# Layernorm scalars and V evictions on ScalarE instead of VectorE, and a second PSUM bank for the Q projection

## Chip, cores and metric

One Trainium2 chip, all 8 cores. The metric is the device time in microseconds of the slowest core, for one launch.

## What is computed

One layer on x of 4 x 4096 x 1024: a layernorm without weights, causal attention with 16 heads of 64, and a gated feed-forward network of hidden size 3072 on the same normalised input, whose output gates the attention's.

```python
def _layernorm(x, axis=-1, eps=1e-5):
    m = jnp.mean(x, axis=axis, keepdims=True)
    v = jnp.var(x, axis=axis, keepdims=True)
    return (x - m) / jnp.sqrt(v + eps)

q = split_heads(x @ Wq) + pos[None, None]
k = split_heads(x @ Wk) + pos[None, None]
v = split_heads(x @ Wv)
scores = jnp.einsum('bhqd,bhkd->bhqk', q, k) * DIM_K ** (-0.5)   # causal mask, softmax
out = jnp.einsum('bhqk,bhkd->bhqd', attn, v)                     # then @ Wo

h = jax.nn.silu(x @ wg.T) * (x @ wu.T)                           # then @ wd.T

xn = _layernorm(x, axis=-1)
s = attention(xn)
g = _silu(ffn(xn))
x = x + s * g
```

## The kernel before

Two cores share one batch element. Each computes 2048 of its 4096 query rows (four blocks of 512, `QBS`, interleaved so that the causal work is alike) and all of its keys and values. Activations are bf16 with the contracted dimension on the partitions; sums are fp32 in PSUM.

The program is a list of instructions for each engine, in an order written out by hand: `P.op(engine, ...)` appends to one engine's list, `waits` names the semaphore counts that it waits for, and each engine runs its list strictly in that order. "T" is TensorE, "V" VectorE, "S" ScalarE, "G" GpSimd's DMA queue, "SY" SyncE's. So an instruction that waits holds up all that stands behind it on its engine. `P.flush` ends a stage.

Stages, in order:
- b0: `ln_phase` normalises the core's 16 own tiles of 128 rows into `xn_own`.
- f1: gate and up projection, with the weights transposed on TensorE. f2: down projection; the gate silu(ffn) goes to HBM by way of `xstA` (`g_spill`).
- b34: `ln_phase` again, for the 32 key/value tiles into `xn_kv`. After each tile a callback, `b34_cb`, appends up to three units of other work from a sorted queue: for each of the 8 head pairs (two heads of 64 are one 128-column pair) four Q units and a last row of squares, and for head pair 0 eight K units, eight norm units, 32 V units and one `u_bound`.
- b5: attention for head pairs 0 to 7. In each pair, block j of four runs over 8, 16, 24 or 32 key chunks of 128 (`EXT`). A chunk c is two score matmuls (`emit_sc`, L916, into bank pair `SC2[c % 2]`), one exp of 128x1024 on ScalarE (L930), on the last four chunks of a block two mask multiplications on VectorE (L944), and, two chunks later, two value matmuls (`emit_av`, L963). After every odd chunk, and after the last `emit_av` of a block, one unit of the next pair's `kv_units` is popped from `fillers`; what is left of them is drained at the end of the pair.
- b6: output projection, gating and residual.

A layernorm tile (`ln_phase`): VectorE sums x (L304) while ScalarE squares it (L307) into a PSUM buffer of 128x1024 that all tiles share (in b34 it is `AV2`); VectorE sums the squares (L310); four VectorE instructions on 128x1 columns of `sLN` give mean, squared mean, mean square and variance (L313 to L322); ScalarE does ln and exp(-0.5 ln) (L325, L328); VectorE makes -mean*rstd (L331) and scales the tile (L335); TensorE transposes it in eight matmuls (L350); ScalarE copies them out in two (L357).

A Q unit (`q_qs`) is eight matmuls of 128x512 into the one bank `Qps[0]` (L609) and an addition of the position table on VectorE (L616); the next unit's first matmul waits for that addition. Each later unit then does `q_sq` for the unit before: squares on VectorE (L627), a matmul with a column of ones (L632), a maximum on VectorE (L641).

A V unit (`emit_vc`) is eight matmuls of 128x128 (L791) into bank c % 2 of `KV2` and a copy of 128x128 to `Vaug` on VectorE (L798). `u_bound` is four VectorE instructions on 1x4 (L811 to L821), four small matmuls (L827) and four additions to the exp's bias table `sBM` (L836), for which the first exp of the next pair waits.

At a block's end ScalarE takes ln and exp(-1) of each head's row of sums (L988, L995), TensorE spreads them (L1002), VectorE copies them (L1011) and multiplies (L1019).

Of the kernel before, what the change touches and what calls it, by code (L numbers as in the profile page):

```python
# [172 lines left out]
def build_program(cfg):  # L173
# [40 lines left out]
    with ExitStack() as top:  # L214
# [55 lines left out]
        def ln_phase(xt_src, ntile, xn_dst, dsem, gates, tag, pool_ext=None,  # L270
                     xnt_ext=None, xnt_gate=None,
                     tp_gate=None, sq_gate=None, interleave_cb=None,
                     tps_ext=None, sqb_ext=None):
            with ExitStack() as ph:
                pe = ph.enter_context
                if pool_ext is not None:
                    xst, xnt = pool_ext
                else:
                    xst = [pe(nc.sbuf_tensor(f"xst{tag}{i}", [128, E], F32))
                           for i in range(2)]  # L280
                    xnt = xnt_ext if xnt_ext is not None else [
                        pe(nc.sbuf_tensor(f"xnt{tag}{i}", [128, E], BF16))
                        for i in range(2)]
                Tps = tps_ext if tps_ext is not None else [
                    pe(nc.psum_tensor(f"Tps{tag}{i}", [128, GT * 128], F32))
                    for i in range(2)]
                sqb = sqb_ext if sqb_ext is not None else pe(
                    nc.psum_tensor(f"sqb{tag}", [128, E], F32))
                xst_free = [None, None]
                sq_free = sq_gate  # L290
                xnt_free = [xnt_gate, xnt_gate]
                tp_free = [tp_gate, tp_gate]
                chain = [None, None]
                last_ev = None
                tile_toks = []
                tctr = 0
                for n in range(ntile):
                    par = n % 2
                    w = [xst_free[par]] + (gates if n < 2 else [])
                    tdma = P.op("SY", ld(xst[par][:], xt_src[n]),  # L300
                                waits=w, inc=dsem[par], amt=16)
                    L = sLN[par]
                    t1 = P.op("V", lambda v, L=L, b=xst[par][:]:
                              v.reduce_sum(L[:, 0:1], b, axis=AX.X),  # L304
                              waits=[tdma, chain[par]], inc="sV")
                    t2 = P.op("S", lambda s, a=sqb[:], b=xst[par][:]:
                              s.activation(a, b, AF.Square),  # L307
                              waits=[tdma, sq_free], inc="sS")
                    t3 = P.op("V", lambda v, L=L, a=sqb[:]:
                              v.reduce_sum(L[:, 1:2], a, axis=AX.X),  # L310
                              waits=[t2], inc="sV")
                    sq_free = t3
                    t4 = P.op("V", lambda v, L=L: v.tensor_scalar(  # L313
                        L[:, 2:3], L[:, 0:1], 1.0 / E, None, ALU.mult),
                        waits=[t1], inc="sV")
                    t5 = P.op("V", lambda v, L=L: v.tensor_tensor(
                        L[:, 3:4], L[:, 2:3], L[:, 2:3], ALU.mult),
                        waits=[t4], inc="sV")
                    t6 = P.op("V", lambda v, L=L: v.tensor_scalar(
                        L[:, 4:5], L[:, 1:2], 1.0 / E, None, ALU.mult),  # L320
                        waits=[t3], inc="sV")
                    t7 = P.op("V", lambda v, L=L: v.tensor_tensor(  # L322
                        L[:, 5:6], L[:, 4:5], L[:, 3:4], ALU.subtract),
                        waits=[t5, t6], inc="sV")
                    t8 = P.op("S", lambda s, L=L: s.activation(  # L325
                        L[:, 6:7], L[:, 5:6], AF.Ln, bias=sCV[:, 0:1]),
                        waits=[t7, tok_consts], inc="sS")
                    t9 = P.op("S", lambda s, L=L: s.activation(  # L328
                        L[:, 7:8], L[:, 6:7], AF.Exp, scale=-0.5),
                        waits=[t8], inc="sS")  # L330
                    t10 = P.op("V", lambda v, L=L: v.tensor_scalar(  # L331
                        L[:, 3:4], L[:, 2:3], L[:, 7:8], -1.0, ALU.mult, ALU.mult),
                        waits=[t9], inc="sV")
                    t11 = P.op("V", lambda v, L=L, a=xnt[par][:], b=xst[par][:]:
                               v.tensor_scalar(a, b, L[:, 7:8], L[:, 3:4],  # L335
                                               ALU.mult, ALU.add),
                               waits=[t10, xnt_free[par]], inc="sV")
# [27 lines left out]

        with ExitStack() as phb0:
# [178 lines left out]
            with ExitStack() as phc:  # L545
# [27 lines left out]
                KV2 = pc(nc.psum_tensor("KV2", [128, max(2 * KVPD, E)], F32))  # L573
                AVps = [AV2[0:65, 0:QBS], AV2[0:65, AVPD:AVPD + QBS]]
                KVp = [KV2[:, 0:KW], KV2[:, KVPD:KVPD + KW]]
                Qps = [SC2[0][:, 0:QW]]
                SQp1 = SC2[0][0:1, 512:512 + QW]
                wq_free = [None, None]
                qps_free = [None]
# [16 lines left out]
                def q_qs(p, qs):  # L596
                    par = p % 2
                    qd = qst[par]
                    last = None
                    for ec in range(EC):  # L600
                        w = [qd["tw"], tok_xnown, qps_free[0]]
                        if p == 0 and qs == 0 and ec == 0:
                            w += [tok_f2S, tok_f1V]
                        last = P.op(
                            "T", lambda t, o=Qps[0][:],
                            l=Wsl[par][:, ec, :],
                            r=xn_own[:, ec, qs * QW:(qs + 1) * QW],
                            st=(ec == 0), sp=(ec == EC - 1):
# [2 lines left out]
                    wq_free[par] = last  # L611
                    tev = P.op("V", lambda v,
                               o=Q_all[:, p, qs * QW:(qs + 1) * QW],
                               a=Qps[0][:],
                               b=sPQ[:, qs * QW:(qs + 1) * QW]:
                               v.tensor_tensor(o, a, b, ALU.add),  # L616
                               waits=[last, tpq], inc="sV")
                    qps_free[0] = tev
                    qd[("tev", qs)] = tev

                def q_sq(p, qs):
# [58 lines left out]
                def kv_units(p, ks, vs, xw):  # L680
# [96 lines left out]
                    def emit_vc(c):  # L777
# [4 lines left out]
                        for ec in range(EC):  # L782
                            w = [kv["twv"], xt, st["kvb"][bi]]
                            if ec == 0:
# [6 lines left out]
                                t.matmul(o, l, r, start=st_, stop=sp),  # L791
                                waits=w,
                                inc="sT" if ec == EC - 1 else None)
                        tev = P.op("V", lambda v,
                                   o=Vaug[par][:, c, :, 0:64],
                                   i_=bank[:, 0:128].rearrange(
                                       "p (two sv) -> p two sv", two=2):
                                   v.tensor_copy(o, i_),  # L798
                                   waits=[last, st["vread"][par]],
                                   inc="sV")  # L800
                        st["kvb"][bi] = tev
                        if c == KVC - 1:
                            st["sl_free"][vs] = last
# [53 lines left out]
                def b34_cb(n, toks):  # L857
                    holder["toks"] = toks
                    c = 0
                    while (qpos[0] < len(b34q) and b34q[qpos[0]][0] <= n  # L860
# [8 lines left out]
                    xnt_ext=[Kp[1][:, i * E:(i + 1) * E]  # L869
                             for i in range(2)],  # L870
                    xnt_gate=tok_f2T,
                    tp_gate=tok_f2S, sq_gate=tok_f1V,
                    tps_ext=[SC2[1][:, 0:GT * 128],
                             SC2[1][:, GT * 128:2 * GT * 128]],
                    sqb_ext=AV2[:, 0:E],
                    interleave_cb=b34_cb)
                while qpos[0] < len(b34q):
                    b34q[qpos[0]][1]()
# [271 lines left out]
```

How the kernel before makes its waits and increments, by code:

```python
            def body(eng):  # L152
                hw = self.hw[qn]
                for fn, waits, inc, amt in ops:
                    for (sn, val) in waits:
                        if val > hw.get(sn, 0):
                            eng.wait_ge(self.sems[sn][0], val)
                            hw[sn] = val
                    ins = fn(eng)
                    if inc is not None:
                        ins.then_inc(self.sems[inc][0], amt)
```

## Time and profile before

| | us |
|---|---|
| median of 2 runs | 2556.6 (2509.32 and 2603.88) |
| the profiled execution | 2511.39 |
| its span, slowest core (core 2) | 2509.8 |
| the other cores' spans | 2493.0 to 2507.1 |

Of the span TensorE matmuls are busy 70%, ScalarE 38%, VectorE 33%. These are means over six stages with different limits, so each stage is to be read by itself. All times of rows below are microseconds from the start of the span, on core 2. The two runs lie 95 us apart; all of what follows is read in, and compared with, the profiled execution, which is like the faster one.

### The profile page before, as it was taken

How to read it: one execution, taken by the hardware profiler on the slowest of the kernel's cores; microseconds unless marked ns; L12 is line 12 of the kernel's file. 1: busy time of each engine (PE TensorE's matmuls, PEld its weight loads, DVE VectorE, ACT ScalarE, POOL GpSimd, SP SyncE). 2: the span in 40 equal slices, each digit the busy share in tenths (PEclk: the TensorE clock that was granted, in tenths of full speed). 3: DMA queues.
4: the chain of work that ended last, by engine and by line, in shares of the span. 5: the costliest groups of instructions: out<-in, count | busy, mean ns of one | idle time of the engine just before them, and what ended most of it. 6: DMA issues, size and time to landing. Idle time of an engine off the chain costs nothing. (4 is left out here: it accounts for less than half of the span.)

```text
span 2509.8 us, 25986 instructions; the slowest of 8 cores (2493.0 to 2509.8 us)
## 1 busy us (share of the span) xinstructions
PE 1748.9 (70%) x8990; PEld 729.5 (29%) x9088; DVE 825.9 (33%) x1746; ACT 958.8 (38%) x1125; POOL 87.4 (3%) x135
## 2 busy tenths in 40 slices
PE   1178888989983444443688777877877787776752
PEld 0134444444431221222223232332323233221211
DVE  4533333330003444444333324233332423321133
ACT  3311111111001111112475665857566584767500
POOL 0011101000000000000000000000000000000000
PEclk9999999999996666665888888988888898888986
DMA  2153433320115121111200000000000000020155
GB/s 77 59 63 39 50 38 47 42 26 34 51 51 88 38 51 42 34 42 42 30 1 5 5 5 4 1 9 1 5 5 5 0 1 1 1 34 1 51 178 173
DMA packets 75135, 89.85 MB, mean 36 GB/s; under 512 B 52994, under 2 KB 53122, under 8 KB 74882
## 3 DMA queue, kind: packets, MB, share of 16 engines
q0 software_dynamic: 62768, 45.62, 11.7%
q1 hardware_dynamic: 12242, 42.57, 5.3%
q8 instruction: 77, 1.26, 0.2%
q14 instruction: 48, 0.39, 0.1%
HBM read 100.24 MB, written 16.78 MB: 47 GB/s over the span
## 5 line engine op out<-in xcount | busy, mean ns | idle before, releaser
L930 ACT ACTIVATE BIG<-SC,sBM 128x1024 bf16<-128x1024 f32 x640 | 683.9, 1111 | 322.5 <-PE SC L916 247.2
L963 PE MATMUL AV<-BIG 128*65 128x512 bf16 x1280 | 421.0, 412 | 87.5 <-DVE BIG L944 36.9
L916 PE MATMUL SC<-BIG 64*128 64x512 bf16 x1280 | 261.8, 414 | 1.3 <-PEq L164 1.3
L488 ACT ACTIVATE sSG<-Gps 128x512 bf16<-128x512 f32 x96 | 57.3, 597 | 378.7 <-PE Gps L474 378.7
L791 PE MATMUL KV<-BIG 128*128 128x128 bf16 x2048 | 182.3, 245 | 25.3 <-DVE BIG L1011 19.9
L474 PE MATMUL Gps<-RA,wgT 128*128 128x512 bf16 x752 | 194.6, 403 | 1.3 <-issue 0.4
L798 DVE CAST BIG<-KV 128x128 bf16<-128x128 f32 x256 | 75.1, 293 | 346.5 <-PE KV L791 343.4
L484 PE MATMUL Ups<-RA,wuT 128*128 128x512 bf16 x744 | 180.4, 381 | 1.3
L963 PEld LDWEIGHTS AV<-BIG 128*65 128x65 bf16 x1280 | 103.2, 115 | 238.9 <-issue 228.9
L350 PE MATMUL SC<-sID,BIG 128*128 128x128 bf16 x256 | 32.4, 306 | 197.4 <-DVE BIG L335 191.5
L528 PE MATMUL Dps<-BIG 128*128 128x512 bf16 x752 | 165.1, 379 | 2.4 <-PEq L164 1.5
L791 PEld LDWEIGHTS KV<-BIG 128*128 128x128 bf16 x2048 | 143.2, 111 | 80.4 <-issue 77.3
L493 DVE TENSOR_TENSOR BIG<-sSG,Ups 128x512 bf16<-128x512 bf16 x96 | 66.0, 688 | 282.2 <-PE Ups L484 278.6
L944 DVE TENSOR_TENSOR BIG<-BIG,sTRI 128x512 bf16<-128x512 bf16 x256 | 97.5, 422 | 177.8 <-ACT BIG L930 177.8
L714 PE MATMUL KV<-BIG 128*128 128x512 bf16 x484 | 142.5, 443 | 19.5 <-DVE BIG L1011 7.8
L916 PEld LDWEIGHTS SC<-BIG 64*128 64x128 bf16 x1280 | 59.6, 94 | 269.4 <-issue 269.3
L325 ACT ACTIVATE sLN<-sLN,sCV 128x1 f32<-128x1 f32 x48 | 14.1, 294 | 313.8 <-DVE sLN L322 313.8
L474 PEld LDWEIGHTS Gps<-RA,wgT 128*128 128x128 bf16 x768 | 77.7, 103 | 94.0 <-issue 15.8
L1092 PE MATMUL OPs<-BIG,RA 128*128 128x512 bf16 x250 | 71.1, 448 | 47.6 <-DVE ot L1109 42.8
L484 PEld LDWEIGHTS Ups<-RA,wuT 128*128 128x128 bf16 x768 | 76.2, 99 | 94.3 <-issue 6.6
L609 PE MATMUL SC<-RA,BIG 128*128 128x512 bf16 x248 | 91.7, 534 | 14.7 <-DMA BIG<-Wq 8.3
L528 PEld LDWEIGHTS Dps<-BIG 128*128 128x128 bf16 x768 | 75.1, 98 | 92.4 <-issue 2.0
(79 smaller groups left out, 1258.5 us busy)
## 6 DMA issues: line engine op xcount, KB each, us to landing
xstA<-x_q SPq DMA_DIRECT2D x32, 512.0 KB, 4.4
xstb<-x_kv SPq DMA_DIRECT2D x32, 512.0 KB, 3.9
g_spill<-xstA POOLq DMA_DIRECT2D x16, 512.0 KB, 2.9
gt<-g_spill POOLq DMA_DIRECT2D x16, 512.0 KB, 5.9
out<-ot SPq DMA_DIRECT2D x16, 512.0 KB, 3.0
wgc<-wg POOLq DMA_DIRECT2D x24, 256.0 KB, 4.0
wuc<-wu POOLq DMA_DIRECT2D x24, 256.0 KB, 5.4
wdc<-wd POOLq DMA_DIRECT2D x24, 256.0 KB, 5.5
```

Of the source, the lines that this page charges most:

```text
L474: t.matmul(o, l, r, start=st, stop=sp),
L484: t.matmul(o, l, r, start=st, stop=sp),
L528: t.matmul(o, l, r, start=st, stop=sp),
L609: t.matmul(o, l, r, start=st, stop=sp),
L714: t.matmul(o, l, r, start=st_, stop=sp),
L791: t.matmul(o, l, r, start=st_, stop=sp),
L798: v.tensor_copy(o, i_),
L916: t.matmul(SC2[bi][:, h * QBS:(h + 1) * QBS], Kp[par][h * 64:(h + 1) * 64, c * 128:(c + 1) * 128], Q_all[h * 64:(h + 1) * 64, p, j * QBS:( ...
L930: s.activation(expb[bi], SC2[bi][:, 0:2 * QBS], AF.Exp, scale=cfg.SM, bias=sBM[par][:, col:col + 1]),
L944: v.tensor_tensor(expb[bi][:, h * QBS:(h + 1) * QBS], expb[bi][:, h * QBS:(h + 1) * QBS], sTRI[:, r * QBS:(r + 1) * QBS], ALU.mult),
L963: t.matmul(AVps[h][:], Vaug[par][:, c, h, :], expb[bi][:, h * QBS:(h + 1) * QBS], start=st_, stop=sp),
L1092: t.matmul(OPs[op][:, ew * EW:(ew + 1) * EW], AO[:, rc, q2 * 128:(q2 + 1) * 128], Wo_sb[:, rc, ew * EW:(ew + 1) * EW], start=st_, stop=sp),
```

## The change

Three edits.

1. In `ln_phase` the five VectorE instructions on 128x1 become ScalarE activations: mean, squared mean, 1e-5 minus the squared mean, mean square, then ln with that difference as its bias, exp, minus the mean, and its product with rstd: six new ScalarE instructions for five VectorE ones. The buffer of squares becomes two, and in b34 they are the SBUF tiles `xstA` (free once the last `g_spill` is stored) and no longer `AV2`.
2. `Qps` has two banks in turn, the second in `AV2`.
3. The copy of a V unit (L798) is a ScalarE copy.

```diff
-                sqb = sqb_ext if sqb_ext is not None else pe(
-                    nc.psum_tensor(f"sqb{tag}", [128, E], F32))
+                sq = sq_ext if sq_ext is not None else [
+                    pe(nc.psum_tensor(f"sqb{tag}{i}", [128, E], F32))
+                    for i in range(2)]
...
-                              waits=[tdma, sq_free], inc="sS")
+                              waits=[tdma, sq_free[par]], inc="sS")
...
-                    t4 = P.op("V", lambda v, L=L: v.tensor_scalar(
-                        L[:, 2:3], L[:, 0:1], 1.0 / E, None, ALU.mult),
-                        waits=[t1], inc="sV")
-                    t5 = P.op("V", lambda v, L=L: v.tensor_tensor(
-                        L[:, 3:4], L[:, 2:3], L[:, 2:3], ALU.mult),
-                        waits=[t4], inc="sV")
-                    t6 = P.op("V", lambda v, L=L: v.tensor_scalar(
-                        L[:, 4:5], L[:, 1:2], 1.0 / E, None, ALU.mult),
-                        waits=[t3], inc="sV")
-                    t7 = P.op("V", lambda v, L=L: v.tensor_tensor(
-                        L[:, 5:6], L[:, 4:5], L[:, 3:4], ALU.subtract),
-                        waits=[t5, t6], inc="sV")
+                    t4 = P.op("S", lambda s, L=L: s.activation(
+                        L[:, 2:3], L[:, 0:1], AF.Copy, scale=1.0 / E),
+                        waits=[t1], inc="sS")
+                    t5 = P.op("S", lambda s, L=L: s.activation(
+                        L[:, 3:4], L[:, 2:3], AF.Square),
+                        waits=[t4], inc="sS")
+                    t5b = P.op("S", lambda s, L=L: s.activation(
+                        L[:, 5:6], L[:, 3:4], AF.Copy, scale=-1.0, bias=1e-5),
+                        waits=[t5], inc="sS")
+                    t6 = P.op("S", lambda s, L=L: s.activation(
+                        L[:, 4:5], L[:, 1:2], AF.Copy, scale=1.0 / E),
+                        waits=[t3], inc="sS")
                     t8 = P.op("S", lambda s, L=L: s.activation(
-                        L[:, 6:7], L[:, 5:6], AF.Ln, bias=sCV[:, 0:1]),
-                        waits=[t7, tok_consts], inc="sS")
+                        L[:, 6:7], L[:, 4:5], AF.Ln, bias=L[:, 5:6]),
+                        waits=[t5b, t6], inc="sS")
...
-                    t10 = P.op("V", lambda v, L=L: v.tensor_scalar(
-                        L[:, 3:4], L[:, 2:3], L[:, 7:8], -1.0, ALU.mult, ALU.mult),
-                        waits=[t9], inc="sV")
+                    ta = P.op("S", lambda s, L=L: s.activation(
+                        L[:, 3:4], L[:, 2:3], AF.Copy, scale=-1.0),
+                        waits=[t9], inc="sS")
+                    tb = P.op("S", lambda s, L=L: s.activation(
+                        L[:, 5:6], L[:, 3:4], AF.Copy, scale=L[:, 7:8]),
+                        waits=[ta], inc="sS")
...
-                Qps = [SC2[0][:, 0:QW]]
+                Qps = [SC2[0][:, 0:QW], AV2[:, 0:QW]]
...
-                        w = [qd["tw"], tok_xnown, qps_free[0]]
+                        w = [qd["tw"], tok_xnown, qps_free[qp]]
...
-                        tev = P.op("V", lambda v,
+                        tev = P.op("S", lambda s_,
                                    o=Vaug[par][:, c, :, 0:64],
                                    i_=bank[:, 0:128].rearrange(
                                        "p (two sv) -> p two sv", two=2):
-                                   v.tensor_copy(o, i_),
+                                   s_.copy(o, i_),
                                    waits=[last, st["vread"][par]],
-                                   inc="sV")
+                                   inc="sS")
...
-                    tp_gate=tok_f2S, sq_gate=tok_f1V,
+                    tp_gate=tok_f2S, sq_gate=gdone,
...
-                    sqb_ext=AV2[:, 0:E],
+                    sq_ext=[xstA[0], xstA[1]],
```

## Rows read from the trace of the kernel before

**Rows 1.** Windows, by stage: window, length, busy us (instructions) per engine, TensorE clock, DMA.
```profile
10.10:134.00 123.90, 16.75 (x134) 12.99 (x135) 61.26 (x128) 41.38 (x81) 4.06 (x6) 1.00 0.26 69
...
751.50:1200.70 449.20, 186.53 (x862) 89.49 (x879) 199.71 (x426) 81.47 (x161) 9.83 (x12) 0.63 0.20 47
1200.70:2363.40 1162.70, 914.77 (x4928) 335.13 (x4948) 363.49 (x888) 759.62 (x769) 13.12 (x15) 0.86 0.05 6
```
**Rows 2.** Groups by line: count, busy us, mean ns of one, idle before.
```profile
L930 ACT ACTIVATE BIG<-SC,sBM 128x1024 bf16<-128x1024 f32 x640 | 683.9, 1111 | 322.5 <-PE SC L916 247.2
L798 DVE CAST BIG<-KV 128x128 bf16<-128x128 f32 x256 | 75.1, 293 | 346.5 <-PE KV L791 343.4
L609 PE MATMUL SC<-RA,BIG 128*128 128x512 bf16 x248 | 91.7, 534 | 14.7 <-DMA BIG<-Wq 8.3
L357 ACT CAST BIG<-SC 128x512 bf16<-128x512 f32 x64 | 34.4, 589 | 69.5 <-PE SC L350 69.5
```
**Rows 3.** Timeline of one layernorm tile in b0: start, length, engine, line.
```profile
47.39 1.23 DVE L310 TENSOR_REDUCE sLN<-sqba 128x1 f32<-128x1024 f32 x1 [1.91 <-ACT sqba L307]
...
49.37 0.29 ACT L325 ACTIVATE sLN<-sLN,sCV 128x1 f32<-128x1 f32 x1 [2.08 <-DVE sLN L322]
49.75 0.20 ACT L328 ACTIVATE sLN<-sLN 128x1 f32<-128x1 f32 x1
...
50.45 0.81 DVE L335 TENSOR_SCALAR BIG<-xstA,sLN 128x1024 bf16<-128x1024 f32 x1 [0.18 <-DVE sLN L331]
```
**Rows 4.** Waits in b34 and in b5: engine, line, releaser, us in total, times, longest.
```profile
PE SC L609 <- DVE BIG L616: 5.2, 5, 1.4
...
ACT BIG L930 <- DVE sBM L836: 73.0, 7, 10.7
```
**Rows 5.** Timeline of b34: second of two adjoining Q units.
```profile
939.35 1.89 PE L609 MATMUL SC<-RA,BIG 128*128 128x512 bf16 x8 [0.95 <-DVE BIG L616]
```
**Rows 6.** Timeline of b34: a V unit ahead of a row of squares.
```profile
803.97 1.06 PE L791 MATMUL KV<-BIG 128*128 128x128 bf16 x8
...
805.13 0.29 DVE L798 CAST BIG<-KV 128x128 bf16<-128x128 f32 x1 [2.23 <-PE KV L791]
...
805.90 0.58 PE L632 MATMUL SC<-BIG,sONE 128*1 128x512 bf16 x1 [0.88 <-DVE BIG L627]
```
**Rows 7.** Timeline of b34's end: the last V unit and u_bound.
```profile
1199.11 0.24 PE L827 MATMUL KV<-sBSB,sOR 1*128 1x1 bf16 x4 [1.46 <-DVE sBSB L821]
```
**Rows 8.** Timeline of attention, two chunks with a V unit (head pair 0).
```profile
1318.04 2.12 ACT L930 ACTIVATE BIG<-SC,sBM 128x1024 bf16<-128x1024 f32 x2 [0.16 <-PE SC L916]
...
1318.87 0.62 PE L791 MATMUL KV<-BIG 128*128 128x128 bf16 x8
...
1320.35 2.12 ACT L930 ACTIVATE BIG<-SC,sBM 128x1024 bf16<-128x1024 f32 x2 [0.19 <-PE SC L916]
```
**Rows 9.** Timeline of attention, the same two chunks without one (head pair 7).
```profile
2263.31 2.12 ACT L930 ACTIVATE BIG<-SC,sBM 128x1024 bf16<-128x1024 f32 x2 [0.16 <-PE SC L916]
...
2265.59 2.12 ACT L930 ACTIVATE BIG<-SC,sBM 128x1024 bf16<-128x1024 f32 x2 [0.16 <-PE SC L916]
```
**Rows 10.** Timeline of a block's end with a V unit.
```profile
1295.19 0.61 PE L791 MATMUL KV<-BIG 128*128 128x128 bf16 x8
1295.45 0.59 ACT L988 ACTIVATE sRCF<-AV 1x512 f32<-1x512 f32 x1 [1.70 <-PE AV L963]
```
**Rows 11.** Timeline of a head pair's end.
```profile
1346.10 1.40 DVE L1019 TENSOR_TENSOR RA<-AV,BIG 64x512 bf16<-64x512 f32 x2
...
1346.14 4.99 PE L791 MATMUL KV<-BIG 128*128 128x128 bf16 x48 [1.72 <-DVE BIG L1011]
...
1351.56 0.22 DVE L811 TENSOR_SCALAR sMK<-sMQ,sMK 1x4 f32<-1x4 f32 x1
...
1352.92 0.23 PE L827 MATMUL KV<-sBSB,sOR 1*128 1x1 bf16 x4 [1.79 <-DVE sBSB L821]
...
1354.05 2.12 ACT L930 ACTIVATE BIG<-SC,sBM 128x1024 bf16<-128x1024 f32 x2 [10.48 <-DVE sBM L836]
```

More of the change, by code:

```diff
@@ L272, in ln_phase @@
                      tp_gate=None, sq_gate=None, interleave_cb=None,
-                     tps_ext=None, sqb_ext=None):
+                     tps_ext=None, sq_ext=None):
             with ExitStack() as ph:
@@ L286, in ln_phase @@
                     for i in range(2)]
-                sqb = sqb_ext if sqb_ext is not None else pe(
-                    nc.psum_tensor(f"sqb{tag}", [128, E], F32))
+                sq = sq_ext if sq_ext is not None else [
+                    pe(nc.psum_tensor(f"sqb{tag}{i}", [128, E], F32))
+                    for i in range(2)]
                 xst_free = [None, None]
-                sq_free = sq_gate
+                sq_free = list(sq_gate) if sq_gate else [None, None]
                 xnt_free = [xnt_gate, xnt_gate]
@@ L305, in ln_phase @@
                               waits=[tdma, chain[par]], inc="sV")
-                    t2 = P.op("S", lambda s, a=sqb[:], b=xst[par][:]:
+                    t2 = P.op("S", lambda s, a=sq[par][:], b=xst[par][:]:
                               s.activation(a, b, AF.Square),
-                              waits=[tdma, sq_free], inc="sS")
-                    t3 = P.op("V", lambda v, L=L, a=sqb[:]:
+                              waits=[tdma, sq_free[par]], inc="sS")
+                    t3 = P.op("V", lambda v, L=L, a=sq[par][:]:
@@ L310, in ln_phase @@
                               v.reduce_sum(L[:, 1:2], a, axis=AX.X),
                               waits=[t2], inc="sV")
-                    sq_free = t3
-                    t4 = P.op("V", lambda v, L=L: v.tensor_scalar(
-                        L[:, 2:3], L[:, 0:1], 1.0 / E, None, ALU.mult),
-                        waits=[t1], inc="sV")
-                    t5 = P.op("V", lambda v, L=L: v.tensor_tensor(
-                        L[:, 3:4], L[:, 2:3], L[:, 2:3], ALU.mult),
-                        waits=[t4], inc="sV")
@@ L319, in ln_phase @@
-                    t6 = P.op("V", lambda v, L=L: v.tensor_scalar(
-                        L[:, 4:5], L[:, 1:2], 1.0 / E, None, ALU.mult),
-                        waits=[t3], inc="sV")
-                    t7 = P.op("V", lambda v, L=L: v.tensor_tensor(
-                        L[:, 5:6], L[:, 4:5], L[:, 3:4], ALU.subtract),
-                        waits=[t5, t6], inc="sV")
+                    sq_free[par] = t3
+                    t4 = P.op("S", lambda s, L=L: s.activation(
+                        L[:, 2:3], L[:, 0:1], AF.Copy, scale=1.0 / E),
+                        waits=[t1], inc="sS")
@@ L330, in ln_phase @@
                         waits=[t8], inc="sS")
-                    t10 = P.op("V", lambda v, L=L: v.tensor_scalar(
-                        L[:, 3:4], L[:, 2:3], L[:, 7:8], -1.0, ALU.mult, ALU.mult),
-                        waits=[t9], inc="sV")
+                    ta = P.op("S", lambda s, L=L: s.activation(
[4 more added lines that the diff above has]
+                        waits=[ta], inc="sS")
                     t11 = P.op("V", lambda v, L=L, a=xnt[par][:], b=xst[par][:]:
-                               v.tensor_scalar(a, b, L[:, 7:8], L[:, 3:4],
+                               v.tensor_scalar(a, b, L[:, 7:8], L[:, 5:6],
                                                ALU.mult, ALU.add),
-                               waits=[t10, xnt_free[par]], inc="sV")
+                               waits=[tb, xnt_free[par]], inc="sV")
                     chain[par] = t11
@@ L575, in build_program @@
                 KVp = [KV2[:, 0:KW], KV2[:, KVPD:KVPD + KW]]
-                Qps = [SC2[0][:, 0:QW]]
+                Qps = [SC2[0][:, 0:QW], AV2[:, 0:QW]]
                 SQp1 = SC2[0][0:1, 512:512 + QW]
                 wq_free = [None, None]
-                qps_free = [None]
+                qps_free = [None, None]
                 sqst = dict(free=[tok_f2T, tok_f2T])
@@ L598, in q_qs @@
                     qd = qst[par]
+                    qp = qs % 2
                     last = None
                     for ec in range(EC):
-                        w = [qd["tw"], tok_xnown, qps_free[0]]
-                        if p == 0 and qs == 0 and ec == 0:
+                        w = [qd["tw"], tok_xnown, qps_free[qp]]
+                        if p == 0 and qs <= 1 and ec == 0:
                             w += [tok_f2S, tok_f1V]
                         last = P.op(
-                            "T", lambda t, o=Qps[0][:],
+                            "T", lambda t, o=Qps[qp][:],
                             l=Wsl[par][:, ec, :],
@@ L613, in q_qs @@
                                o=Q_all[:, p, qs * QW:(qs + 1) * QW],
-                               a=Qps[0][:],
+                               a=Qps[qp][:],
                                b=sPQ[:, qs * QW:(qs + 1) * QW]:
@@ L617, in q_qs @@
                                waits=[last, tpq], inc="sV")
-                    qps_free[0] = tev
+                    qps_free[qp] = tev
                     qd[("tev", qs)] = tev
```

## The prediction

> **What bounds the kernel now.** I read four views, in this order. The windows by stage [rows 1] show that only three of the six stages hold any edited line: b0 (124 us), b34 (449 us) and b5 (1163 us). In b0 and b34 no engine is near full: in b34 VectorE is busy 200 of 449 us, TensorE 187, ScalarE 81, and TensorE's granted clock is 0.63. Such a stage is a chain that passes from engine to engine, so a term is worth the time it takes out of the chain, not the busy time that it moves. In b5 TensorE is busy 915 and ScalarE 760 of 1163 us. The groups by line [rows 2] give the price of one instruction, the list of waits [rows 4] says where an engine really stood still, and the timelines [rows 3, 5 to 11] say what would start earlier if it did not.
>
> In attention two chunks take 2.27 to 2.31 us, with a V unit [rows 8] and without [rows 9], and ScalarE rests only 0.16 to 0.19 of it. So the beat is the loop exp, value matmuls, scores, next exp; the V unit on TensorE costs nothing there, and ScalarE has almost no room. That is where edit 3 puts 140 copies.
>
> **Edit 1, the scalars.** In the chain of a tile [rows 3] the sum of squares starts at 47.39 and ln at 49.37: 1.98 us. After: the sum itself 1.23, a hand-over of 0.10 (the gap between L325 and L328 is 0.09), the mean square on ScalarE 0.20 (as L328, also 128x1), 0.10: 1.63. The other three new instructions ahead of it run while VectorE sums (3 x 0.3 = 0.9, under 1.23); if that sum were not there they would cost 0.9. From exp's end (49.95) to the scaling (50.45) it is 0.50; after, 0.10 + 0.20 + 0.10 + 0.29 (a scale read from a column, priced as L325, which reads its bias from one) + 0.10 = 0.79. Net -0.06 a tile. If the last costs 0.20 it is -0.15, and if all cost 0.29 it is +0.12: for 48 tiles -7 to +6 us. I take 0. VectorE loses work, but nothing on it waits for these instructions but the chain itself. The second buffer of squares gives nothing: the next square already stands behind this tile's copies on ScalarE. Its gate on the stored gates is long open when the first x tile lands.
>
> The Trainium skill's page "ScalarE: Activation LUTs", section "Rules for kernel authors", speaks against this edit: plain adds and multiplications belong on VectorE. By it alone each tile would get longer; by the rows seven small instructions in series (L313 to L331) become five, since three now run beside the sum of squares, and that pays for dearer ones. No sum above hangs on it.
>
> **Edit 2, the second Q bank.** TensorE waited for the Q eviction 5 times, 5.2 us in all [rows 4], one of them 0.95 us [rows 5]. In the written order this can happen only where a pair's first two Q units adjoin in one tile, which is so for 5 of 8 pairs. In every other case the row of squares between two Q units makes TensorE wait anyway, longer than the eviction lasts. I take all of it, -5.2; nothing is the other end.
>
> The Trainium skill's page "Perfetto Trace Analysis", section "Matmuls", says that independent matmul groups should rotate through PSUM banks so that an eviction overlaps the next group. Read so, each of 32 Q units would gain. The rows allow five; this is a rival below.
>
> **Edit 3, the V copy, in b34.** VectorE now waits in line for the V unit's matmuls and keeps the squares behind it waiting: V matmuls end at 805.03, copy at 805.13, then squares, and TensorE gets its row of squares at 805.90, after 0.88 us idle [rows 6]. After, the squares are done before, and the matmul follows at once. The order has six such places: 6 x -0.88 = -5.3. Where the V unit is a tile's last, the new chain is copy and square on ScalarE, the old one copy and sum of x on VectorE; about as long, so 0. At the stage's end `u_bound` no longer queues behind the copy: TensorE's 1.46 us of waiting [rows 7] goes, -1.4.
>
> **Edit 3 in attention.** 224 copies (7 pairs x 32). In the written order 26 of each pair's 32 V units fall into blocks 2 and 3, and 6 are drained. What a copy costs on ScalarE no row shows. From 0.20 for one column [rows 3] and 0.589 for 512 [rows 2], 128 columns are 0.20 + (127/511) x 0.39 = 0.30. Two exps take 2.12, not 2 x 1.111 [rows 2, 8]: adjoining instructions overlap by 0.10. So a copy takes 0.20 of ScalarE.
> - Steady chunks, 20 a pair, 140 in all. Exp is done at 1320.16, the V matmuls at 1319.49; the copy slips in at 1320.06 and the next exp may start at 1320.26, while its scores let it start only at 1320.35. Cost 0, margin 0.06 to 0.09 us. If nothing overlaps, the copy takes 0.30 plus two hand-overs of 0.10 less the 0.16 to 0.19 gap, about 0.3 us a time: 42 us. Ends 0 and +42; I take 0, because exps, and L357's two, do overlap although each has a wait.
> - Masked chunks, 4 a pair: ScalarE idles there, 0.
> - Ends of blocks 2 and 3, 14 in all. ln of the sums starts at 1295.45, before the unit's matmuls end at 1295.80 [rows 10]. After, the copy stands ahead of it: 1295.90, and ln at about 1296.1 to 1296.3. ScalarE's four activations set the start of the next block, so all of it counts: +0.7 (0.65 to 0.85) x 14 = +9.8. It is the only sure cost.
> - Ends of pairs, 7. Exp of the next pair stood 73.0 us in 7 waits for `sBM` [rows 4], 10.5 each. In it TensorE finishes the V matmuls at 1351.13 (1346.14 + 4.99), VectorE is still copying until 1351.56, then does L811 to L821, and TensorE's L827 comes at 1352.92 [rows 11]. After, those four instructions run from 1347.5 (when L1019 is through) to about 1348.8, under the V matmuls, and L827 follows them at 1351.13: 1.79 us x 7 = -12.5.
>
> **Sum.** 0 - 5.2 - 5.3 - 1.4 + 0 + 9.8 - 12.5 = -14.6 us. On the profiled execution's 2511.4 (span 2509.8 and 1.6 around it) that is 2496.8, so 2497 us, 0.6% less. It stands 60 us under the shown median of 2556.6, which lies between two runs 95 us apart; my figure is for an execution like the faster one, 2509.3, and a change of 15 us is less than the 2% that a measurement of this kernel can tell from no change.
>
> **Rivals.**
> - *ScalarE becomes attention's pace* (the other sign). Each of the 140 copies lengthens its beat. For: the margin is under 0.1 us in 2.27. Against: the overlap that the exps show. It outweighs all gains once a copy costs 0.10 us beyond its margin (14.6 / 140); at 0.30 the time is 2539, slower by 28 us. Chance 0.2, spread from 2511 to 2539.
> - *The layernorm chain gets longer.* +0.12 to +0.2 for 48 tiles, and half the gain of edit 2 missing: 2497 + 10 + 3 = 2510. For: each new instruction is dearer than the one it replaces. Against: there are five in the chain where there were seven. Chance 0.13.
> - *TensorE's clock rises.* In b34 the granted clock is 0.63, and L609's matmuls show a mean of 534 ns [rows 2], between a fast and a slow level; in attention it is 0.86. A fast set of eight took 1.89 us [rows 5]; at half the clock I estimate 3.6. If a half of the roughly 20 slow sets of 32 turned fast, since idle gaps between them go, that is 10 x 1.7 = 17 us: 2480. If the gaps removed at the pairs' ends did the same for the slow matmuls behind them, 2455. Against: the 5 us of layernorm in which TensorE does nothing stay in every tile. Chance 0.12.
> - *Rotation of banks pays for all Q units*, 27 more x 0.95 = 26 us: 2471. Against: the list of waits. Chance 0.05.
> - *As summed*, 2485 to 2505. Chance 0.5.
>
> **How the numbers follow.** The range 2470 to 2530 holds the summed case, the chain case, the bank case, most of the clock case and the first's up to 0.23 us a copy; it leaves out some 0.1 to 0.15 at the ends. Faster by over 2% is under 2461: only the far end of the clock case, 0.07 with what I may have missed. Slower by over 2% is over 2562: beyond even the full price of the copies, 0.04. Within 2%: 0.89.
>
> **What would show it.** Right: L798 on ScalarE at 0.26 to 0.30 us; two steady chunks with a V unit still at 2.27 to 2.31; the wait of L930 for `sBM` at 60 us, not 73; the wait of L609 for L616 gone; ln at a block's end 0.7 later; b0 at 124 us, b34 at about 437, b5 at about 1160. Wrong: a beat of 2.4 or more in blocks 2 and 3, or b5 above 1175 (the first rival); b0 above 130 (the second); a granted clock in b34 of 0.7 or more (the third); a table load between copies and exps on ScalarE, of which the trace has none inside a stage now and which I take to stay so.

## The result, and the profile after

The changed kernel takes 2474.3 us (median of 9 runs, 2471.5 to 2480.2), the kernel before 2512.4 us (median of 8) beside it on the same chip. The ratio is 0.985, with a 95% interval from 0.983 to 0.986: 38 us less, where 14.6 less were forecast. The time itself lies inside the forecast's range of 2470 to 2530. On this chip a few executions of any kernel have one half of the cores at a lower clock; they are left out of all ratios, and for the kernel with two fills below, whose profile is such a one, the stage times are means of the four cores of the other half (the kernel before has 448.3 and 1159.4 there).

Both changed stages gave more than their terms. The mean over the eight cores of one profiled execution each:

| stage | before | after | difference | forecast |
|---|---|---|---|---|
| b34 | 448.2 | 428.7 | -19.5 | -11.9 |
| of it TensorE idle | 258.5 | 244.6 | -13.9 | |
| of it TensorE busy | 189.8 | 184.1 | -5.7 | 0 |
| b5 | 1159.0 | 1142.5 | -16.5 | -2.7 |
| of it TensorE idle | 242.5 | 240.0 | -2.5 | |
| of it TensorE busy | 916.5 | 902.4 | -14.1 | 0 |

The other stages are as they were. Busy and idle are split because the number of matmuls and their shapes are the same in both kernels: if TensorE is busy for less time, each matmul ran faster, and that is its clock. The split is not exact, since a faster matmul where ScalarE sets the pace only turns into idle time, but it says where to look. Lines of the changed kernel stand five further down than in [rows 1 to 11] from the Q unit on (L930 is L935), and one to four further down in the layernorm. The idle lines are nearly the forecast; the busy lines were forecast as nothing.

The windows by stage on core 2, b34 and then b5, as in [rows 1] (after the busy times of TensorE, its weight loads, VectorE, ScalarE and GpSimd come the granted TensorE clock, the DMA share and GB/s):
```profile
751.10:1182.50 431.40, 182.50 (x860) 89.35 (x876) 170.97 (x234) 131.89 (x385) 9.86 (x12) 0.64 0.21 49
1182.50:2326.30 1143.80, 902.59 (x4928) 331.04 (x4948) 300.32 (x664) 801.69 (x993) 13.15 (x15) 0.87 0.05 6
```
The granted clock is 0.01 higher in each than in [rows 1]; that is little to look at, and it carries half of the result.

The end of a head pair, changed kernel, core 2, TensorE alone (start, length; in brackets the idle time before and what ended it), which answers to [rows 11]:
```profile
1326.79 4.59 PE L796 MATMUL KV<-BIG 128*128 128x128 bf16 x48 [1.72 <-DVE BIG L1016]
1331.31 0.25 PE L832 MATMUL KV<-sBSB,sOR 1*128 1x1 bf16 x4
1331.49 0.61 PE L921 MATMUL SC<-BIG 64*128 64x512 bf16 x4
1334.13 0.59 PE L968 MATMUL AV<-BIG 128*65 128x512 bf16 x2 [2.03 <-ACT BIG L935]
...
1336.20 1.67 PE L719 MATMUL KV<-BIG 128*128 128x512 bf16 x7 [0.16 <-issue]
1337.72 0.59 PE L968 MATMUL AV<-BIG 128*65 128x512 bf16 x2
```
and the same place in the kernel before, from behind the bound's matmuls at 1352.92 [rows 11]:
```profile
1353.08 0.61 PE L916 MATMUL SC<-BIG 64*128 64x512 bf16 x4
1355.31 1.04 PE L963 MATMUL AV<-BIG 128*65 128x512 bf16 x2 [1.62 <-ACT BIG L930]
...
1358.76 2.68 PE L714 MATMUL KV<-BIG 128*128 128x512 bf16 x7 [0.33 <-issue]
1361.27 0.59 PE L963 MATMUL AV<-BIG 128*65 128x512 bf16 x2
```
The 1.79 us ahead of the bound's matmuls are gone, as forecast. What was not forecast stands behind them: the same pair of value matmuls takes 0.59 us where it took 1.04, and seven matmuls of the first K unit take 1.67 where they took 2.68. From the start of the drained V matmuls (1326.79; 1346.14 before) to the value matmuls behind the K unit it is 10.9 us, not 15.1. The windows of these stretches on core 2 (the granted clock is the third number from the end), first the kernel before, then the changed one:
```profile
1346.14:1351.13 4.99, 4.99 (x48) 4.61 (x48) 2.80 (x7) 0.00 (x0) 0.00 (x0) 0.56 0.01 3
1353.00:1361.40 8.40, 6.45 (x24) 1.98 (x25) 0.70 (x4) 4.35 (x4) 0.00 (x0) 0.59 0.32 31
```
```profile
1326.82:1331.50 4.68, 4.62 (x54) 4.35 (x55) 1.98 (x6) 1.38 (x6) 0.00 (x0) 0.66 0.01 4
1331.50:1339.20 7.70, 5.42 (x30) 1.82 (x28) 1.80 (x5) 4.94 (x6) 0.88 (x1) 1.00 0.35 34
```
While V units are drained the granted clock is 0.56 and 0.66, nearer to the lower of its two levels (1.2 GHz, shown as 0.5) than to the upper (2.4 GHz, shown as 1.0), though TensorE is busy nearly throughout: before them lies a block's end, where in the kernel before it was busy for 1.0 of 4.7 us. Behind them the changed kernel has the upper level (1.00), the kernel before 0.59.

This pair's end on core 2 is of the better half; core 7 has 0.78 at the same place of the changed kernel. So here is the granted clock of the 8.4 us from the bound's first matmul on, over all 7 pair ends of all 8 cores (28 ends for the kernel with two fills), for the kernels that the experiments below explain:

| kernel | mean clock behind the bound | ends at 0.99 or more |
|---|---|---|
| before | 0.59 | 0 of 56 |
| changed | 0.90 | 28 of 56 |
| changed, late bound | 0.60 | 0 of 56 |
| before, one fill | 0.86 | 20 of 56 |
| before, two fills | 1.00 | 28 of 28 |
| before, bound early | 0.86 | 28 of 56 |

### The profile page after: what moved, and what is told of

Same layout as the page of the kernel before. It is cut to its first block and busy times, and to the rows that moved or that the text cites. A ratio compares the mean times of both kernels' runs of the same rounds, so it can differ in the third digit from the quotient of the medians.

```text
span 2472.5 us, 26122 instructions; the slowest of 8 cores (2455.7 to 2472.5 us)
## 1 busy us (share of the span) xinstructions
PE 1741.6 (70%) x9088; PEld 725.1 (29%) x9088; DVE 723.2 (29%) x1250; ACT 1071.9 (43%) x1669; POOL 87.4 (4%) x135
## 5 line engine op out<-in xcount | busy, mean ns | idle before, releaser
L935 ACT ACTIVATE BIG<-SC,sBM 128x1024 bf16<-128x1024 f32 x640 | 684.0, 1113 | 214.4 <-PE SC L921 204.0
L796 PE MATMUL KV<-BIG 128*128 128x128 bf16 x2048 | 180.3, 244 | 24.2 <-DVE BIG L1016 18.6
L488 PE MATMUL Ups<-RA,wuT 128*128 128x512 bf16 x768 | 183.2, 382 | 0.0
L968 PEld LDWEIGHTS AV<-BIG 128*65 128x65 bf16 x1280 | 102.3, 114 | 241.5 <-issue 231.3
L803 ACT CAST BIG<-KV 128x128 bf16<-128x128 f32 x256 | 68.6, 268 | 145.8 <-PE KV L796 145.8
L726 DVE TENSOR_TENSOR BIG<-KV,sPK 128x512 bf16<-128x512 f32 x64 | 44.2, 690 | 167.0 <-PE KV L719 167.0
L354 PE MATMUL Tpsa<-sID,BIG 128*128 128x128 bf16 x128 | 16.2, 307 | 105.8 <-DVE BIG L339 105.8
```

Of the source, the lines that this page charges most:

```text
L488: t.matmul(o, l, r, start=st, stop=sp),
L803: s_.copy(o, i_),
L935: s.activation(expb[bi], SC2[bi][:, 0:2 * QBS], AF.Exp, scale=cfg.SM, bias=sBM[par][:, col:col + 1]),
L968: t.matmul(AVps[h][:], Vaug[par][:, c, h, :], expb[bi][:, h * QBS:(h + 1) * QBS], start=st_, stop=sp),
```

## The experiments

Two theories. **Theory A**, that of the forecast: the waits taken out and put in add up, and the clock is as it was. **Theory B**: shorter standing of TensorE also lets its clock rise sooner, and the matmuls behind the gap run at the higher level. Stage times below are means over the eight cores of the profiled execution; microseconds of the whole are (1 - ratio) x 2508, the median of the kernel before on these chips.

| kernel | ratio to before, 95% interval | whole | b34: time, TensorE busy, idle | b5: time, TensorE busy, idle |
|---|---|---|---|---|
| before | 1 | | 448.2, 189.8, 258.5 | 1159.0, 916.5, 242.5 |
| changed | 0.9847, 0.983 to 0.9864 | -38 | 428.7, 184.1, 244.6 | 1142.5, 902.4, 240.0 |
| edit 1 alone | 0.9983, 0.9973 to 0.9993 | -4 | 447.3, 189.7, 257.6 | 1158.0, 916.1, 241.9 |
| edit 2 alone | 0.9963, 0.9946 to 0.998 | -9 | 440.6, 187.4, 253.2 | 1158.7, 917.0, 241.7 |
| edit 3 alone | 0.9885, 0.986 to 0.991 | -29 | 434.6, 183.2, 251.4 | 1140.4, 900.2, 240.2 |
| edit 3, attention only | 0.9945, 0.9925 to 0.9965 | -14 | 451.7, 192.6, 259.1 | 1144.5, 903.1, 241.5 |
| changed, late bound | 0.9964, 0.995 to 0.9978 | -9 | 428.9, 184.0, 245.0 | 1169.4, 918.6, 250.8 |
| before, two fills | 0.9921, 0.9904 to 0.9937 | -20 | 448.9, 190.4, 258.6 | 1128.9, 898.8, 230.1 |
| before, one fill | 0.9934, 0.9912 to 0.9957 | -17 | 448.3, 190.7, 257.6 | 1141.3, 904.6, 236.8 |
| before, fills in b34 | 0.9968, 0.9956 to 0.9979 | -8 | 437.1, 196.0, 241.1 | 1158.6, 916.7, 241.9 |
| before, bound early | 0.9902, 0.9874 to 0.9931 | -25 | 448.8, 190.5, 258.3 | 1135.6, 899.5, 236.1 |
| changed, block ends back | 0.9819, 0.9799 to 0.9838 | -45 | 429.5, 184.3, 245.2 | 1132.2, 899.1, 233.0 |
| and squares ahead | 0.9698, 0.9679 to 0.9718 | -76 | 429.3, 184.1, 245.2 | 1097.9, 894.4, 203.5 |
| and one fill | 0.9642, 0.9623 to 0.9661 | -90 | 429.4, 183.7, 245.7 | 1089.5, 892.5, 197.0 |

**The edits one by one.** Edit 1 alone is the changed kernel with edits 2 and 3 taken back:
```
- Qps = [SC2[0][:, 0:QW], AV2[:, 0:QW]]
+ Qps = [SC2[0][:, 0:QW]]          # and qp = 0
- tev = P.op("S", ... s_.copy(o, i_), ... inc="sS")
+ tev = P.op("V", ... v.tensor_copy(o, i_), ... inc="sV")
```

> Edit 1 alone: the layernorm scalars on ScalarE and the two buffers of squares; one Q bank, V copies on VectorE. Theory A (the removed and added waits simply add up, TensorE's clock stays): 0 us against the kernel before, b0 and b34 as before (about 124 and 448 us). Theory B (the removed idle of TensorE also makes later matmuls run at the fast level): also 0, since the tile's chain keeps its length, 8.3 us a tile. A third reading, that edit 1 is part of b34's gain of 19.5 us after all: -5 to -7 here, with tiles of 8.15 us.

-4 us (2 to 7 by the interval), of which b34 and b5 show 1 each: little, but not nothing, and no single profile says where the rest lies. The third reading of the expectation is out, since single tiles of b34 still take 8.28 us. One tile of the chain in b0, changed kernel, core 7, as [rows 3]:
```profile
47.35 1.22 DVE L311 TENSOR_REDUCE sLN<-sqba 128x1 f32<-128x1024 f32 x1 [1.91 <-ACT sLN L314]
...
48.67 0.20 ACT L323 ACTIVATE sLN<-sLN 128x1 f32<-128x1 f32 x1 [0.71 <-DVE sLN L311]
48.97 0.30 ACT L326 ACTIVATE sLN<-sLN 128x1 f32<-128x1 f32 x1
49.35 0.20 ACT L329 ACTIVATE sLN<-sLN 128x1 f32<-128x1 f32 x1
49.65 0.20 ACT L332 ACTIVATE sLN<-sLN 128x1 f32<-128x1 f32 x1
49.95 0.30 ACT L335 ACTIVATE sLN<-sLN 128x1 f32<-128x1 f32 x1
50.42 0.81 DVE L339 TENSOR_SCALAR BIG<-xstA,sLN 128x1024 bf16<-128x1024 f32 x1 [1.84 <-ACT sLN L335]
```
From the sum of squares to the scaling it is 3.07 us, before it was 3.06 (47.39 to 50.45). The two buffers of squares, a part of edit 1, stay in all four kernels with a part of the change, so no run has them apart from the others. Edit 2 alone has the second bank, and t4 to t10 of the layernorm as before (t4, t5, t6, t7 and t10 on VectorE):

> Edit 2 alone: the second Q bank (the squares of x move to SBUF so that the bank is free; the scalars stay on VectorE). Theory A: -5.2 us, all in b34 (448 to 443), b5 as before (1159). Theory B: -5.2 and about 1.7 us more for each slow set of eight Q matmuls that turns fast; of b34's measured -19.5 it takes up to -8 here (b34 at 440), b5 as before.

b34 falls by 7.6 us, 5.3 of them idle time (the forecast term was 5.2) and 2.4 matmul time. Edit 3 alone has one bank, the old layernorm scalars and the copy on ScalarE:

> Edit 3 alone: the V copy on ScalarE in b34 and b5. Theory A: -5.3 - 1.4 + 9.8 - 12.5 = -9.4 us (b34 -6.7, b5 -2.7). Theory B: about -30 us (b34 -12 to -14, b5 -16), since the slow K matmuls after a pair's end turn fast.

b34 falls by 13.6 us (idle 7.1, forecast 6.7; busy 6.6) and b5 by 18.6 (idle 2.3, forecast 2.7; busy 16.3). This is theory B's figure, and the edit carries most of the change. With the copies moved in attention only (`"V" if p == 0 else "S"`):

> The V copy on ScalarE for pairs 1 to 7 only, that is in attention; pair 0's copies in b34 stay on VectorE, and so do the scalars; one Q bank. Theory A: b34 448 as before, b5 +9.8 - 12.5 = -2.7 us, total -2.7. Theory B: b34 448, b5 -16 us, total -16.

b5 -14.5, theory B again. b34 reads 3.5 us longer than before although no copy in it is moved; its eight cores lie between 446.7 and 456.3, and the 7.4 us between two of them (core 3, 454.1, and core 5, 446.7) arise ahead of the eighth tile's scaling. So one profile fixes b34 to no better than some 3 us. The three edits alone add up to -42 us (4 + 9 + 29) beside -38 together, with the two buffers of squares counted three times.

**The gap at a pair's end, put back.** In the changed kernel `u_bound` waits for the last V copy again:
```
  t1 = P.op("V", ... waits=[kv["rm_tok"], tok_mq[p]]
+                         + ([kv["lastv"]] if p > 0 else []), inc="sV")
```


> The changed kernel, but the four VectorE instructions of u_bound wait for the last V copy again (pairs 1 to 7), so that TensorE stands at a pair's end before the bound's matmuls as it did in the kernel before. TensorE's idle time in b5 goes from 240 back up by about 12.5 us in both theories. Theory A (waits add up, clock untouched): b5 1142.5 + 12.5 = 1155, total 2474 + 12.5 = 2487, TensorE's busy time in b5 stays 902. Theory B (the gap at the pair's end is what keeps the clock low behind it): besides the 12.5 the busy time goes back to about 916, b5 to 1165 or more, total 2497 to 2501.

TensorE's idle time in b5 rises by 10.8 us, the busy time by 16.2 us to 918.6, the stage by 26.9. The whole goes from 0.9847 to 0.9964 of before, 29 us. The seven gaps are 14.5 us on core 2, a little more than the 12.7 of before. The windows by stage, core 2, b5:
```profile
1182.90:2354.00 1171.10, 916.52 (x4928) 334.14 (x4950) 300.83 (x664) 801.18 (x993) 13.12 (x15) 0.86 0.05 6
```
The clock is 0.86 again, as in [rows 1], and 0.60 behind the bound. b5 is now 10.4 us above the kernel before: the block ends, made later by the copies, stand there with nothing to pay for them (9.8 in the forecast). The median is 2498 us; theory A had 2487, theory B 2497 to 2501.

**The gap filled and nothing removed.** The kernel before, with matmuls that compute nothing where TensorE stands. First in two places at a pair's start: four matmuls in the 1.8 us gap ahead of the bound's matmuls, as below, and four more into `KVp[1]` behind the first two score pairs. Then only in the gap:
```
+ if p > 0:
+     for i_ in range(4):
+         P.op("T", ... t.matmul(SC2[1][:, 512:1024], xn_kv[:, 3, 0:128],
+                                xn_kv[:, 4 + i_, 0:512], ...),
+              waits=[st["sc2"][1]])
  lastb = None          # the bound's matmuls
```


> The kernel before, nothing of the change in it, but 4 + 4 matmuls of 512 columns that compute nothing at each start of pairs 1 to 7: four ahead of the bound's matmuls, four behind the first two score pairs, both in time in which TensorE stands and nobody waits for it. Theory A: they can only cost, 0 to +5 us; b5 1159 to 1164. Theory B: the clock is high when the first K unit comes, so b5 falls by 8 to 14 us to 1145 to 1151, though no wait was removed; total 2498 to 2504 beside 2510.

> The kernel before with four matmuls of 512 columns that compute nothing in just the gap of 1.8 us at a pair's end that the change removes (ahead of the bound's matmuls, pairs 1 to 7), none behind the score pairs. Theory A (waits add up, clock untouched): 0 to +2 us. Theory B (this gap is what keeps the clock low for the K unit behind it): at least a half of the 14 us of matmul time that the change saved in b5 comes back, b5 1159 to about 1145 to 1150, total -8 to -14. If it gives nothing while the version with both fills gave -20, it is the longer standing behind the score pairs that matters.

-20 and -17 us for work that is of no use. Timeline of a pair's end in the kernel with one fill, core 2. L825 is the fill (one of the four has no record), L834 the bound's matmuls, L923 scores, L970 value matmuls, L714 the K unit:
```profile
1349.95 0.81 PE L825 MATMUL SC<-BIG 128*128 128x512 bf16 x3
...
1351.69 0.23 PE L834 MATMUL KV<-sBSB,sOR 1*128 1x1 bf16 x4 [0.92 <-DVE sBSB L821]
1351.85 0.61 PE L923 MATMUL SC<-BIG 64*128 64x512 bf16 x4
...
1354.08 0.59 PE L970 MATMUL AV<-BIG 128*65 128x512 bf16 x2 [1.62 <-ACT BIG L937]
...
1356.38 3.03 PE L714 MATMUL KV<-BIG 128*128 128x512 bf16 x8
```
The bound's matmuls still wait for VectorE, and the exp still follows as before; only the first value matmuls take 0.59 us, not 1.04. At this end the clock does not hold: the K unit still takes 3.03 us, and the 8.4 us have 0.80. Over all ends they have 0.86, and 1.00 with both fills. Without the fills (28 matmuls, 6.8 us, whose records overlap their neighbours' a little) TensorE is busy 898.6 us in b5, 17.9 less than before. This is the cause by itself, and it is more than the 14 us that were missing. Both runs gave more than theory B had asked for (8 to 14 us of b5; it fell by 30.5 and 17.7), so its size was put too low.

The same in b34, two matmuls ahead of each of the 32 rows of squares:

> The kernel before with two matmuls of 512 columns that compute nothing ahead of each of the 32 row matmuls of squares in b34 (L632 in the kernel before), in time in which TensorE stands 1.1 us in the mean and no one waits for it. Theory A: 0 to +5 us, since the extra matmuls never end before the squares do. Theory B: the gaps in b34 are filled, so Q and K matmuls behind them are faster: b34 448 to 435 to 442, b5 unchanged at 1159, total -6 to -13. A third reading (b34's clock is held down by the 5 us of layernorm in each tile alone): nothing, 448.

b34 falls by 11.1 us, inside theory B's range, and b5 stays. The fill is busy 24.5 us there, all other matmuls 177.2, 12.6 less than before. (The two overlap by 5.7 us in the trace: TensorE's 196.0 less the 24.5 would give too large a gain.) Groups by line, b34, core 2 (count, busy us, mean ns of one):
```profile
L609 PE MATMUL SC<-RA,BIG 128*128 128x512 bf16 x247 | 82.6, 490 | 13.0 <-DMA BIG<-Wq 6.8 <-DVE BIG L616 4.8 <-issue 1.3
...
L631 PE MATMUL SC<-RA 128*128 128x512 bf16 x62 | 23.9, 472 | 0.9 <-DVE BIG L803 0.6 <-issue 0.2
```
A Q matmul takes 490 ns where [rows 2] had 534, with 4.8 of the 5.2 us of the wait for the Q eviction [rows 4] still there. L631 is the fill.

**The same gap removed without the move.** In the kernel before, the four small VectorE instructions of `u_bound` are issued behind the last norm unit, ahead of the V copies, which stay on VectorE:
```
  kv["rm_tok"] = kv["rm_tok2"]
+ if p > 0 and kg == NKG - 1:
+     u_bscal()         # t1, t2, t2b, t3; u_bound uses its token
```


> The kernel before; nothing moves to ScalarE, the V copies stay on VectorE. Only the four small VectorE instructions of u_bound are issued right behind the last norm unit instead of behind the last V copy (pairs 1 to 7). The wait at a pair's end goes as in edit 3, and the block ends are not made later. Theory A: b5 -12.5, 1159 to 1146.5, total -12.5. Theory B: the 12.5 and some 14 us of matmul time: b5 to about 1132, total -24 to -28, the same as the changed kernel with its block-end copies put back (1132.2).

b5 -23.4: idle 6.4, busy 17.0. Edit 3 alone gained 18.6 us in b5 with its block ends made later, this gains 23.4 without touching them. The idle time falls by less than the 12.5 us of the gaps, since matmuls that run faster where ScalarE sets the pace leave new idle time.

**Block ends.** The changed kernel with the V copy of the unit at a block's end on VectorE (attention's other copies stay on ScalarE; the value matmuls then wait for the last copy of either engine):
```
+ st["on_v"] = True
  if fillers:
      fillers.pop(0)()      # the unit behind a block's last value matmuls
+ st["on_v"] = False
...
- tev = P.op("S", ...)
+ on_v = st.get("on_v", False)
+ tev = P.op("V" if on_v else "S", ...)
```

> The changed kernel, but the V copy of the unit that stands at the end of a block (behind its last value matmuls, ahead of ln) is on VectorE again; all others stay on ScalarE. Theory A: the 0.7 us that ln lost at 14 block ends comes back, -9.8 us against the changed kernel: 2464, b5 1133, TensorE's busy time 902 as before. Theory B says the same of the wait; a change in the busy time of more than 3 us would say that this wait, too, acts on the clock. Rival: ln was held up by something else as well (its own value matmuls), then under -4 us.

b5 -10.3 beside the changed kernel, against 9.8 forecast; idle 7.0 of it, busy 3.3. The whole falls by 7 us. The kernel with the bound early and no copy on ScalarE has b5 at 1135.6, this one at 1132.2: the copies that stay on ScalarE cost nothing that shows. And on top of it the squares of a K group, in pairs 1 to 7, one unit ahead of their row matmul:
```
  tsq = P.op("V", ... square of group kg ...)
- tmm = P.op("T", ... row matmul of group kg ...)
+ if kg > 0: u_norm2(kg - 1, kv["tsq"])   # row matmul and maximum, one behind
+ if kg == NKG - 1: u_norm2(kg, tsq)      # the last group at once
```


> As the run before it, and the squares of a K group (L742 in the kernel before) are issued one unit ahead of their row matmul (pairs 1 to 7), which takes away most of the 54 us in b5 in which TensorE stands before that matmul; the clock is 0.5 to 0.8 there now. Theory A: only the part of the 54 us that sets the pace comes back, about half, since the mask and the exps are near behind: -20 to -30 us against the run before it, busy time of TensorE in b5 unchanged. Theory B: the busy time falls too, by 7 pairs x some 15 slow matmuls x 0.2 = 20 us or more: -40 to -50 us in all.

The wait of the row matmul for its squares in TensorE's list of waits, core 2, in the changed kernel and in this one (total us, times, longest; b34's 7.9 are in both):
```profile
PE KV L754 <- DVE BIG L747: 62.2, 26, 2.6
```
```profile
PE KV L766 <- DVE BIG L749: 7.9, 5, 1.8
```
b5 falls by another 34.3 us, idle 29.5 and busy 4.7. Here theory B was too bold (it had 20 us of busy time): most of this gain is the wait itself. The whole is 30 us below the run before it. With one fill of four matmuls into `KVp[1]` behind the first two score pairs as well, as in the kernel with two fills:

> The best version so far (block-end V copies on VectorE, squares of a K group one unit ahead; 0.9698 of the kernel before) with four matmuls of 512 columns that compute nothing behind the first two score pairs of pairs 1 to 7. Theory A: 0.970, nothing changes. Theory B: in this version the K unit behind a pair's start is mostly fast already, so there is less to gain than in the kernel before: 0.965 to 0.970.

0.9642, just under theory B's 0.965 to 0.970: b5 8.4 us less, and the clock behind the bound 1.00 at all ends, where it was 0.91 without the fill. This is the best version measured, 3.6% below the kernel before and 2.1% below the changed one.

## Why the forecast was wrong

It said -14.6 us and the time fell by 38. **The sum of waits held in the main.** TensorE's idle time fell by 13.9 us in b34 and 2.5 in b5, together 16.4, against 14.6 in the sum. That b5's 2.5 so nearly met the forecast's 2.7 is in part luck: putting the pair ends' gaps back added 10.8 us of idle time, not 12.5, and taking the block ends' delay away removed 7.0, not 9.8, so in idle time the terms were about 2 and 3 us smaller, with opposite signs, and the errors cancelled. **The step that failed** is the one that left TensorE's clock as it was, with a chance of 0.12 for a rise. The matmul time fell by 5.7 + 14.1 = 19.8 us, and no term of the sum held that: each gap at a pair's end was priced at its own 1.79 us, and the slow matmuls behind it at nothing. The runs show their part at 14 us in the changed kernel and 16 to 18 where the gap alone was changed.

- *Edit 1, 0 us:* near; alone it gave -4, 2 to 7 by the interval, and the chain does not show it. New instructions took 0.20 and 0.30 us as priced, the shortest tiles of b34 8.27 to 8.34 us against 8.29. The Trainium skill's page "ScalarE: Activation LUTs", section "Rules for kernel authors", gives multiplications to VectorE; the trace shows neither gain nor loss from going against it here (3.06 us and 3.07): the chain has two links fewer, which pays for its dearer ones.
- *Edit 2, -5.2:* right as a wait (5.3 idle alone), and 2.4 us of matmul time short. That all Q units would gain from the rotation did not show: it would have been -31 in place of -5.
- *Edit 3 in b34, -5.3 and -1.4:* right as waits (7.1 idle in edit 3 alone), 6.6 us short.
- *140 steady copies, 0:* right. Two chunks with a V unit, changed kernel, core 7:
```profile
1288.89 2.12 ACT L935 ACTIVATE BIG<-SC,sBM 128x1024 bf16<-128x1024 f32 x2
...
1290.91 0.27 ACT L803 CAST BIG<-KV 128x128 bf16<-128x128 f32 x1
...
1291.20 2.12 ACT L935 ACTIVATE BIG<-SC,sBM 128x1024 bf16<-128x1024 f32 x2
```
  The period is 2.31 us as in [rows 8]; the copy takes 0.27 (0.30 priced) and fills the gap in which ScalarE rested, so the margin is all but used up. The rival in which ScalarE becomes the pace fell.
- *Block ends, +9.8:* right, 10.3 when put back. On core 7 ln starts 1.00 us behind the start of the unit's matmuls, where [rows 10] has 0.26, so 0.74 later (forecast 0.7):
```profile
1274.50 0.61 PE L796 MATMUL KV<-BIG 128*128 128x128 bf16 x8
1275.20 0.27 ACT L803 CAST BIG<-KV 128x128 bf16<-128x128 f32 x1 [1.98 <-PE KV L796]
1275.50 0.59 ACT L993 ACTIVATE sRCF<-AV 1x512 f32<-1x512 f32 x1
```
- *Pair ends, -12.5:* the wait went as forecast (no idle ahead of L832), but the place gave about twice that. With the block ends' 9.8 taken off, b5's -16.5 is -26.3 in gross, 3.8 us a pair instead of 1.79; the rest is the clock.
- *The observable "the wait of L930 for `sBM` at 60 us, not 73"* misled: L935 shows 7.1 us in the changed kernel, since ScalarE now does copies in that time, which cut its idle time into pieces. With the bound early and the copies left on VectorE the same wait is 59.9 us. What matters is when the exp starts after the drained matmuls begin: 1346.14 to 1354.05 before, 7.9 us, and 1326.79 to 1332.87 after, 6.1.

**What the forecast could have read.** The rival named the very mechanism: "If the gaps removed at the pairs' ends did the same for the slow matmuls behind them, 2455." Its "against" was the 5 us of layernorm in each tile, and these are in b34 alone; for b5 there was none. The trace of before shows at the pair's end value matmuls of 1.04 us between others of 0.59, and a clock of 0.59 in the 8.4 us behind the gap and 1.00 after. That is the place where a gap of 1.79 us was to be taken out. With that the case deserved more than one in eight. Its price was too high: from 2480 to 2455 it gave the pairs' ends 25 us, and 17 to b34, where the changed kernel shows 14 and 5.7.

The Trainium skill's page "TensorE: Matmul & The Clock Gate", section "HAM oscillation — how this bites in real kernels", says that stalls between bursts of matmuls bring the clock down and that what follows runs slowly. The traces agree: 0.59 behind the gap, 0.90 without it, and 17 us back when only the gap was filled. The page's stalls are longer than this one; that a gap of 1.79 us behind a block's end counts is shown by the runs here.

What stays open: why the squares one unit ahead brought so little clock (4.7 us of busy time for 29.5 of idle time) when 32 fills in b34 brought 12.6 us; no run separates the places within a block. That b34's 5.7 us of busy time in the changed kernel come from its shorter waits is argued: its Q matmuls on core 2 do run faster (123 at 557 ns and 125 at 485, so 521 in the mean, against 534), and the fills show that filled waits have such an effect, but no run shows it place by place.

## What to carry to other kernels

Price a wait of TensorE twice: once for itself, and once for the matmuls that follow it, by looking whether they run slow now and whether the clock of the next stretch is below 1. If they do, the second part can be larger than the first (16 us of matmul time beside 11 of idle time when the gap was put back). Before moving work to another engine to free a queue, try to issue the few small instructions that others wait for ahead of it: here that alone gave 25 us, where moving all V copies gave 29, and it makes no block end later.

## What was not expected of the hardware

Matmuls that compute nothing made the kernel faster: 28 of them in a gap of 1.8 us at 7 places gave 17 us, 64 of them, busy for 24.5 us, shortened b34 by 11. And a TensorE that is busy without a break is not at its full clock for that: the drained V matmuls run 4.99 us on end at a granted 0.56, behind a block's end in which it had mostly stood.
